# A graph network kernel's first stage: products regrouped between the count chunks, two operand tiles earlier, zeros on another engine

## The reference

```python
x = _layernorm(x + gated_gcn(x))    # x1 = x @ W1 + b1 (1024 -> 512), then 4 gate steps, [x1 | result]
x = _layernorm(x + sage(x))         # two mean aggregations with W_self, W_neigh
x = _layernorm(x + attention(x))
x = _layernorm(x + gcn(x))
# one gate step of the first layer
alpha = tanh(x_i @ gw[:D] + x_j @ gw[D:] + gb)
msg = dis[row] * dis[col] * alpha * x_j          # dis = degree ** -0.5
out = segment_sum(msg, col)
```

## Time and profile before

| what | value |
|---|---|
| median of 3 runs | 1545.11 us (1543.84 to 1545.37) |
| the profiled execution's own time | 1544.58 us |
| its span, first to last instruction | 1542.7 us |
| TensorE busy | 1517.8 us (98%) |
| VectorE busy | 885.7 us (57%) |
| ScalarE busy | 752.0 us (49%) |
| GpSimd busy | 184.3 us (12%) |
| granted TensorE clock, mean | 0.998 |

### The profile page before, as it was taken

How to read it: one execution, slowest core, us unless ns; L and a number is a source line. 1 busy time by engine, 2 the same in 40 slices (tenths; PEclk the granted TensorE clock), 3 DMA queues, 4 the chain that set the end, 5 groups by cost and what they waited for, 6 DMA issues and landing times.

```text
span 1542.7 us, 19256 instructions
## 1 busy us (share of the span) xinstructions
PE 1517.8 (98%) x6985; PEld 1221.9 (79%) x6985; DVE 885.7 (57%) x1413; ACT 752.0 (49%) x1358; POOL 184.3 (12%) x306
## 2 busy tenths in 40 slices
PE   6999999999999999999999999999999999999997
PEld 5877877878887888788878777888888778877776
DVE  9878788887645343422433344567598356436346
ACT  6567667768733343333332234335597236533233
POOL 0110021324300000000000000212143013100003
PEclk9999999999999999999999999999999999999999
DMA  5333153325774433433344424564466248545236
GB/s 193 110 108 134 34 180 118 110 77 187 259 253 159 145 115 128 147 107 138 110 171 128 147 78 145 189 230 162 147 182 194 89 145 296 189 131 172 94 120 185
DMA packets 103198, 231.75 MB, mean 150 GB/s; under 512 B 23162, under 2 KB 25972, under 8 KB 103096
## 3 DMA queue, kind: packets, MB, share of 16 engines
q1 hardware_dynamic: 89996, 191.54, 38.6%
q10 hardware_dynamic: 13100, 38.86, 6.6%
HBM read 170.98 MB, written 59.37 MB: 149 GB/s over the span
## 4 chain that ended last, share of the span: by engine, by line
PE 95%; DVE 3%; ACT 1%; issue 0%; POOLq 0%; DVEq 0%; ACTq 0%
PE bank L986 18%; PE bank L842 15%; PE bank L844 15%; PE bank L843 15%; PE bank L997 9%; PE bank L990 9%; PE bank L988 9%; PE bank L1072 2%; PE bank L912 1%; PE bank L880 1%; DVE oK L1782 1%; ACT Tt L1156 0%; DVE Zl L1505 0%; DVE wl L1426 0%; DVE Tt L1464 0%
## 5 line engine op out<-in xcount | busy, mean ns | idle before, releaser
L842 PE MATMUL bank<-wh,xh 128*125 128x512 f32 x1032 | 415.4, 403 | 0.5 <-DVE G L1716 0.5
L843 PE MATMUL bank<-wl,xh 128*125 128x512 f32 x1040 | 410.5, 395 | 0.0
L844 PE MATMUL bank<-wh,xl 128*125 128x512 f32 x1040 | 409.8, 394 | 0.0
L986 PE MATMUL bank<-Zh,Mh 125*125 125x512 f32 x990 | 396.5, 400 | 1.0 <-ACT Mh L1138 1.0
L1438 DVE TENSOR_TENSOR xl<-xs,xh 128x1000 fp32r<-128x1000 f32 x130 | 155.5, 1198 | 291.0 <-ACT xh L1121 290.7
L1121 ACT CAST xh<-xs 128x1000 fp32r<-128x1000 f32 x130 | 132.9, 1026 | 303.2 <-PE bank L844 290.8
L997 PE MATMUL bank<-Zl,Mh 125*125 125x512 f32 x590 | 232.6, 394 | 0.0
L844 PEld LDWEIGHTS bank<-wh,xl 128*125 128x125 f32 x1040 | 193.2, 186 | 48.7
L843 PEld LDWEIGHTS bank<-wl,xh 128*125 128x125 f32 x1040 | 193.3, 186 | 44.3
L842 PEld LDWEIGHTS bank<-wh,xh 128*125 128x125 f32 x1032 | 191.3, 185 | 45.2 <-issue 0.8
L986 PEld LDWEIGHTS bank<-Zh,Mh 125*125 125x125 f32 x990 | 184.0, 186 | 45.8 <-ACT Mh L1138 1.1
(11 more groups left out here) (186 smaller groups left out, 1832.0 us busy)
## 6 DMA issues: line engine op xcount, KB each, us to landing
xs<-xT_d SPq DMA_DIRECT2D x80, 500.0 KB, 3.6
Ar<-a_d SPq DMA_DIRECT2D x100, 312.5 KB, 3.3
xs<-hT_d SPq DMA_DIRECT2D x40, 500.0 KB, 3.5
x_d<-XO ACTq DMA_DIRECT2D x30, 512.0 KB, 5.1
R<-x_d SPq DMA_DIRECT2D x60, 256.0 KB, 4.3
xT_d<-XT ACTq DMA_DIRECT2D x30, 500.0 KB, 3.6
ws<-in_W SPq DMA_DIRECT2D x30, 256.0 KB, 3.6
Tt<-m_d SPq DMA_DIRECT2D x10, 625.0 KB, 5.6
```

Source lines behind the costliest of these rows:

```text
L842: te.matmul(o, xh[i % 2][:, k, :], wh[s][:], start=(k == 0), stop=False)
L843: te.matmul(o, xh[i % 2][:, k, :], wl[s][:], start=False, stop=False)
L844: m = te.matmul(o, xl[i % 2][:, k, :], wh[s][:], start=False, stop=(k == 7))
L986: te.matmul(o, Mh[i][:, s, :], zh, start=(n == 0), stop=False)
```

## The change

Three edits are made. `X_AT` puts the parts of x1 in quarters and halves of a tile: the parts of tile 0 stand two by two, those of tiles 1 to 7 four by four, each group where its first part stood. All that is derived from `X_AT` moves with it: `X_END` goes from [32, 52, 71, 90, 109, 129, 148, 167] to [30, 44, 64, 83, 102, 121, 141, 160], and with it `x1_post`, `second` and `slab`. The groups of four stand behind the chunks 35, 44, 54, 64, 73, 83, 93, 102, 112, 121, 131, 141, 150 and 160. ScalarE makes `Zh` of tiles 0 and 1 behind count tile 5 and of tile 2 behind count tile 6 (all three stood behind count tile 7), and VectorE makes `Zl` of these three behind the keys 134, 137 and 155 (150, 155 and 160 before). The four pad-row memsets go from VectorE to GpSimd, through a view of the same 1250 two-byte elements as one packed row of bf16.

```diff
@@ -37,7 +37,9 @@
 X0_AT = [2 * k for k in range(8)]
 X_FROM = 16
 X_UNITS = 64
-X_AT = [X_FROM + u * (NC - X_FROM) // X_UNITS for u in range(X_UNITS)]
+X_AT = [X_FROM + (u - u % (2 if u < 8 else 4)) * (NC - X_FROM) // X_UNITS for u in range(X_UNITS)]
+
+Z_AT = (134, 137, 155)
 X_END = [X_AT[8 * n + 7] for n in range(8)]
@@ -1355,9 +1357,11 @@
-                if t == 7:
-                    for d in range(3):
+                if t == 5:
+                    for d in range(2):
                         z_first(d)
+                if t == 6:
+                    z_first(2)
@@ -1732,9 +1736,6 @@
             def prologue():
                 ve.memset(zz[:], 0.0).then_inc(s_zz, 1)
-
-                for t in AF16 + AT16:
-                    ve.memset(t[96:128, :, :], 0.0).then_inc(s_pad, 1)
                 q.wait_ge(s_pool0, 1)
@@ -1801,8 +1802,8 @@
-                        if c in (150, 155, 160):
-                            d = (150, 155, 160).index(c)
+                        if c in Z_AT:
+                            d = Z_AT.index(c)
                             z_lower(d, d, G[:, d, :], DIS)
@@ -1999,6 +2000,10 @@
             chain("p", po.memset(half[:], -0.5))
             mine()
+
+            for i, t in enumerate(AF16 + AT16):
+                po.memset(t[96:128, :, :].rearrange("p a c -> p (a c)").bitcast(bf), 0.0).then_inc(s_pad, 1)
+                q.wait_ge(s_pad, i + 1)
             rsqrt_degrees(0, 5, 1)
```

More of the change, by code:

```diff
@@ L1827, in build @@
                                                  ALU.add, ALU.is_equal).then_inc(gS, 1)
+                        if t == 5:
+                            degrees(0, 5)
                         if t < 8:
@@ L1831, in build @@
                             x1_post(t)
-                        if t == 5:
-                            degrees(0, 5)
                         if t == 8:
```

## The result

The changed kernel takes 1547.91 us (median of 20 runs, 1546.22 to 1549.95), the kernel before 1545.26 us (median of 20, 1542.56 to 1547.04) in the same session. The ratio is 1.0022, interval 1.0015 to 1.0028. So it is slower, by an amount that lies at the 0.2% from which a measurement tells a change: 2.65 us between the medians and some 3.4 by the ratio, where the forecast said 1.7. The time lies in the stated range and just inside the forecast's own narrower one (1544.4 to 1548.0). The profiled execution took 1549.52 us with a span of 1547.7.

The account below looks back on a forecast made before the run. TensorE was taken as the bound, with VectorE having only 13% to spare. The terms -2.1 - 1.8 - 1.4 + 7.0 gave +1.7 us on the profiled 1544.58, so 1546.3 us, range 1541.6 to 1548.7.

Parts of the forecast that it names:

- Opening, -2.1: Start of the kernel: without VectorE's memsets, off moves from 7.07 to 4.9 us and later keys follow; -2.1 us, bounds -1.1 and -3.0.
- the sum stays at none: Opening: GpSimd's memsets were counted as slowing VectorE by nothing; one blocked instruction would lose at most 1.2 us.
- Boundaries, -1.8: Chunk stage on TensorE: 46 fewer changes between parts and chunks at 0.04 us each; -1.8 us, bounds 0 and -4.1.
- not all of the 0.09 comes back: A part behind a chunk takes 0.32 us against 0.23; about 0.04 of the 0.09 was counted as saved.
- a shorter L844 on average: Sign for x1's part products: shorter on average, since three of four stand behind another part; no size given.
- Z sooner, -1.4: Around 91 to 97 us: earlier Zh removes VectorE's 2.42 us wait and TensorE's 1.36 us idle; -1.4 us.
- New waits, +7.0: Chunk stage: TensorE waits for keys behind groups ending tiles (6.0 us) and at the degrees (1.75); +7.0 taken, bounds 0 and 9.
- G would wait about 2 us behind each group: Sign on VectorE: behind each group that ends a tile, G waits about 2 us for TensorE.
- Tail, nothing: From the last chunk to the first gate product: moves with TensorE's own order, so no gain or loss.
- the keys do run out (the first): Chunk stage; the rival said keys don't run out, with new waits under 2.2 us filling VectorE's slack; chance 0.22.
- The clock (the second): Rival at the degrees, behind chunk 94: 1.75 us of close idle drops the clock; 1548.1 us for one drop; chance 0.16.
- The small opening (the third): Rival at the start: ei or a blocked instruction holds VectorE, only 1.1 us is gained, giving 1547.3 us; chance 0.12.

Follow-up runs that it names:

- zeros_only: The kernel before with only the four pad memsets moved from VectorE to GpSimd: ratio 0.9989 to the kernel before.
- spread_words: The kernel before with Z sooner and the pad memsets on GpSimd as four-byte elements, parts spread as before: ratio 0.9981 to the kernel before.
- groups_only: The kernel before with the new X_AT alone, parts in twos and fours, Z and memsets as before: ratio 1.0037 to the kernel before.
- after_no_z: The changed kernel with Zh and Zl put back where they stood before: ratio 1.0028 to the kernel before.
- post_degrees_later: The changed kernel with both moves: x1_post nine keys later and degrees(0, 5) behind key 104 instead of 98: ratio 0.9980 to the kernel before.
- post_later: The changed kernel with x1_post(n) nine keys later, behind key X_END + 17: ratio 1.0014 to the kernel before.

## Why the forecast was too low, step by step

The measured time lies in the range given, above the forecast, and the sum behind the forecast has terms that were wrong in both directions. By the first gate product, where the terms can be separated, it is +3.58 against +1.7. The mechanism that the forecast put first, VectorE's end-of-tile work behind a group, is the one that the experiments show; two gains were put too high, by 1.0 and 1.8 us, and three smaller errors (0.3, 0.2 and 0.4) happened to lie the other way.

- **Opening, -2.1: measured -1.1.** `off` at 4.9 was right (4.92), and the price of a memset on GpSimd nearly so (1.14 against 1.2). The step that failed is "the sum stays at none" on GpSimd slowing VectorE: `hi` stood still beside a memset for 1.03 us. By the Trainium skill (SBUF — State Buffer, Who interferes with whom) a `tensor_scalar` in a two-port mode and a GpSimd instruction exclude each other for the whole of it; the trace agrees (1.27 and, in `zeros_only`, 1.16 us for what takes 0.24 and 0.25 alone). The row of the select beside a VectorE memset, on which I set the cost to none, was of another kind of instruction and said nothing of this one. (That same select takes 0.40 us in the changed kernel, where a `tensor_scalar` runs beside it, and 0.29 before; no run isolates this.) The trace of before did hold a sign, far outside the stage that was read: at 214.81 us a VectorE product waits for a GpSimd addition, as shown at the end. With the memsets short enough to end ahead of `hi`, the first chunk comes 2.20 sooner than before (`spread_words`), so the -2.1 was what the move to GpSimd could give.
- **Boundaries, -1.8: measured none.** Here "not all of the 0.09 comes back" should have been: nothing does. My 9.0 us for a tile was a sum of rounded starts with an error as large as the difference that I drew from it. The sign that I named for it, a shorter L844 on average, came true (417 against 486 ns) and proved nothing.
- **Z sooner, -1.4: measured -1.7 on the old spread, and 0 on the groups.** The wait at 96.73 does vanish in the changed kernel, but `groups_only` and `after_no_z` show that the groups remove it by themselves. The 1.7 us therefore stay in the sum below, though they are not earned by the Z edit.
- **New waits, +7.0: measured +6.8** (80.66 less the 73.82 of the kernel with both moves). The places and the order of size are as written: 1.3 foreseen and 1.04 and 1.06 of idle for tiles 1 and 2, 0.85 and 0.50 for tile 3, 0.75 and 0.35 for tile 4, 0.9 and 0.72 and 0.75 for 5 and 6, 0.95 and 0.8 against 0.76 and 0.67 at the degrees. The idle time alone is less than the cost: 5.56 of the 6.84, the rest 1.28, or 0.16 for each wait. In stride a TensorE record ends about 0.16 us after the next one has started, and idle time is counted from that end, so a wait costs about that much more than its idle time; counting from start to start, as the prediction did, includes it. The sign that G would wait about 2 us behind each group was too high: it waited 0.63 to 1.15, and not at all for tile 4.
- **Tail, nothing: measured -0.4.** Behind the last chunk TensorE waited 0.55 us for VectorE's G before the change. This wait is gone in the groups, since x1's tile 7 ends sooner (behind chunk 160 and not 167); I had taken the tail as moving with the chunks alone.

The sum of what was measured: -1.1 + 0 - 1.7 + 6.8 - 0.4 = +3.6.

Of the rivals, the keys do run out (the first), though `post_degrees_later` shows that they need not: VectorE's slack is enough when its waits are placed for it. The clock (the second) did not fall at the degrees, 1.00 from 60 to 80 us, with 1.43 us of idle there; it did in `post_later` with 3.3. The small opening (the third) came true, and at its price of 1.1 us.

**Open.** The profiled execution of the changed kernel is another 1.4 us behind by 260 us, lost from 205 us on, in steps that the change does not touch. TensorE idles 1.53 us there against 0.60, waiting for VectorE, whose products stand behind GpSimd's additions eight times against six (shown at the end). The additions start when a transfer lands. Executions of both kernels spread by about 4 us, so this isn't put down to the change. Nor is it settled what tips the clock at 128 us: before and after have a granted clock of 0.91 from 120 to 140 us (the lower level for 3.4 us), and `after_no_z` has 1.00 there with the same two waits of TensorE (0.94 and 0.77 us). Of the fourteen profiled executions five have this drop and nine do not. All of this lies behind the first gate product, which is why that is the better measure.

## What to carry to other kernels

When products are gathered into groups on the engine that is the bound, look at what the other engine does when a group ends: work that waits for the group must stand so far behind it in that engine's order that the wait is over, and all such pieces must move together, since moving one alone can put two in a row. A product whose row gets shorter has gained nothing until the distance from start to start over the whole stretch is shorter. Before giving an idle engine small work at the start, see which instructions of its neighbour run meanwhile, look through the whole trace for places where the two engines overlap already, and make that work short in elements.

## What the runs showed of the hardware

- A VectorE `tensor_scalar` of 125x170 (int32 or f32 in, f32 out) takes 0.24 us alone and 1.15 to 1.27 behind the last GpSimd memset, ending 0.11 us after it (6.90 and 7.01 in the changed kernel and in `zeros_only`). One that starts in the last 0.1 us of a memset (5.62 us in `after_no_z`, the memset ending at 5.70) takes its 0.24. The `tensor_tensor` `off` (0.34 us at 4.92) and the custom instruction behind it ran beside the same memsets with no loss.
- A GpSimd memset takes 1.14 us for 1250 elements of two bytes and 0.62 for the same bytes as 625 words, and the next one starts 0.06 later.
- Two-input work on both engines excludes each other too. Rows of the changed kernel, a VectorE product with GpSimd idle and one behind a GpSimd addition:

```profile
180.40 1.46 DVE L1468 TENSOR_TENSOR Tt<-Tt,Ar 125x1250 f32<-125x1250 f32 x1 [0.76 <-ACT Tt L1158]
...
211.54 1.65 POOL L1953 TENSOR_TENSOR U<-R 128x512 f32<-128x512 f32 x1 [2.08 <-DMA R<-in_x]
...
212.11 2.39 DVE L1468 TENSOR_TENSOR Tt<-Tt,Ar 125x1250 f32<-125x1250 f32 x1
```

  The addition ends at 213.19 and the product 1.32 us later, at 214.50. All eight products of the changed kernel that start 0.2 to 0.8 us behind such an addition, from 204 to 260 us, end 1.32 after its end, whether they then take 1.82 or 2.42. In the kernel before, six do the same, and in these two rows the product is first:

```profile
201.20 1.46 DVE L1464 TENSOR_TENSOR Tt<-Tt,Ar 125x1250 f32<-125x1250 f32 x1 [1.77 <-ACT Tt L1156]
202.10 1.72 POOL L1952 TENSOR_TENSOR U<-R 128x512 f32<-128x512 f32 x1 [82.52 <-DMA R<-in_x]
```

  Here the product keeps its 1.46 and the addition takes 1.72 where most take 1.29. So whichever comes second stands until the first is done. These are readings of the traces; no run removes the additions.
